# Two interleaved decoder streams on one core: another merged order of the steps, another table of constant matmuls

## The chip, the cores and the metric

The kernel runs on one core of a Trainium2 chip. The metric is the device time of one execution in microseconds, lower is better. A core has five engines that run their own instruction lists in order and meet through semaphores: TensorE (PE in the profile, its weight loads PEld), VectorE (DVE), ScalarE (ACT), GpSimd (POOL) and SyncE (SP), which here only issues transfers.

## The reference, cut to what matters

Two post-norm decoder layers over x of 4 x 512 x 256 in f32. Each batch row goes through six sublayers, each followed by a residual sum and a layer norm:

```python
x = _layernorm(x + _L0_attn_ref(x, Wk, Wq, Wv))                  # causal softmax attention
x = _layernorm(x + _L0_xattn_ref(x, ctx, ctx, mask, ...))        # masked cross attention, own norm
x = _layernorm(x + _L0_ffn_ref(x, k0, k1, k2, s0, s1, s2))       # three dense layers of +1/-1 weights
x = _layernorm(x + _L1_attn_ref(x, Wqkv, ..., proj))             # performer: relu features, causal sums
x = _layernorm(x + _L1_xattn_ref(x, ctx, ctx, Wi_w, ...))        # mLSTM: gated, decayed scores
x = _layernorm(x + _L1_ffn_ref(x, w1, conv_w, conv_b, w2))       # quantized dense, conv over tokens, silu, dense
```

The batch rows are independent of one another. Only the weights are shared.

## The kernel before

**Streams and rounds.** The four batch rows are worked on as two streams, a and b, in two rounds: stream a takes rows 0 and 2, stream b rows 1 and 3. Each stream has its own buffers and its own four of the eight PSUM banks. A third program, p, prepares the weights (on POOL and SP it is called w).

**Programs and steps.** On each engine a stream is a Python generator that yields the name of a step and then emits its instructions. The names are the sublayer and the tile: `self.*` and `cross.*` (the attentions; for each of four row tiles `score`, `turn`, which transposes the probabilities, and `product`), `sign.*` (the dense layers: `sign.xT`, `sign.a0` to `a7`, `sign.b0` to `b7`, `sign.c0` to `c3`), `perf.*` (performer), `mlstm.*` and `quant.*` (the last sublayer: `quant.turn`, `row1`, `hidden0` to `hidden7`, `taps`, `topT`, `row2`, `down0` to `down3`). DVE takes row maxima, norms, half of the bank reads and all of the rounding; ACT takes the exponentials, silu and the other bank reads.

**The order.** `weave` merges the programs of an engine by a table: "a11 b2 a7" means eleven steps of a, two of b, seven of a. There is a table for each engine, so the instruction order of every engine is written out by hand or by a planner outside of this file:

```python
for turn in turns.split():
    name = turn[0]
    for _ in range(int(turn[1:])):
        ahead[name] = next(programs[name], None)
```

There are 590 steps on PE, 773 on DVE, 522 on ACT, 101 on POOL and 34 on SP. Every engine runs its steps strictly in this order, so a step whose inputs are late holds all that stands behind it, of the other stream too.

**The preparing steps.** `prep.scales` on DVE waits for all four transfers of the sign weights (`sign_in`) and then makes their scale and sign columns in eight small instructions (L1221 to L1235); after four of them it signals `signs_taken`. `prep.w10` to `prep.w17` on ACT (L1831) wait for `sign_in` and `signs_taken` and turn one of eight slices of weights from bytes into f16; `prep.w2` (L1834) is four more such instructions. `prep.w00` and `w01` on DVE do the same for the first layer.

```python
dve.wait_ge(*sign_in.all())
dve.wait_ge(*rows_in.all())
```

**The start of stream a.** PE: `self.q` (L564), `self.v` (L572), `self.score0` (L598, L600), `self.cv0` (values of the cross attention, L572), `self.score1`, `self.turn0` (L607). ACT copies the results of `self.q` (L1876) and of `self.v` (L1881) out of their banks; the banks of `self.v` are those that `self.score1` and `self.turn0` write next. DVE takes the row maximum of a score tile (L1276), ACT then its exponential (L1806 loads the table, L1851), and PE turns it.

**Constant matmuls.** `claim` stands ahead of most PE steps. It waits for the bank and then runs as many 128x512 bf16 matmuls of constants (L550) as the table `KEEP` has for that step. Their result is overwritten by the step itself:

```python
for _ in range(KEEP.get(f"{name} {s.index} {n}", 0)):
    nc.tensor.matmul(u.bank[:, :], identb[:, :], ..., start=True, stop=True)
```

The key is step, stream (0 for a, 1 for b) and round.

## Time and profile before

| what | value |
|---|---|
| time of the runs, median of 3 | 808.02 us (807.7 to 809.53) |
| profiled execution, span from the first to the last instruction | 808.1 us |
| PE matmul busy | 738.1 us, 91% of the span |
| DVE busy | 560.4 us, 69% |
| ACT busy | 347.2 us, 43% |
| mean granted TensorE clock | 0.976 of full |
| TensorE at half clock | six stretches, among them 418.0 to 421.4 us and 721.8 to 732.0 us |

The profile gives no time of its own for the profiled execution beside its span; the span is within 0.1 us of the median of the runs. In the profile a line such as L1276 is a line of the kernel. Both streams and both rounds share the lines, so a step is found by the order of the instructions in the timeline, not by the line alone. The granted clock is a share of full speed: 1.00 is 2.4 GHz, 0.50 is 1.2 GHz.

### The profile page before, as it was taken

How to read it: one execution, taken by the hardware profiler on the slowest of the kernel's cores; microseconds unless marked ns; L12 is line 12 of the kernel's file. 1: busy time of each engine (PE TensorE's matmuls, PEld its weight loads, DVE VectorE, ACT ScalarE, POOL GpSimd, SP SyncE). 2: the span in 40 equal slices, each digit the busy share in tenths (PEclk: the TensorE clock that was granted, in tenths of full speed). 3: DMA queues.
4: the chain of work that ended last, by engine and by line, in shares of the span. 5: the costliest groups of instructions: out<-in, count | busy, mean ns of one | idle time of the engine just before them, and what ended most of it. 6: DMA issues, size and time to landing. Idle time of an engine off the chain costs nothing.

```text
span 808.1 us, 14850 instructions
## 1 busy us (share of the span) xinstructions
PE 738.1 (91%) x5976; PEld 485.7 (60%) x5976; DVE 560.4 (69%) x1405; ACT 347.2 (43%) x640; POOL 166.7 (21%) x249
## 2 busy tenths in 40 slices
PE   9999999989999978689979999999999998978494
PEld 6776565667657745557744576867656676646242
DVE  1558436575457589997899973647546569799887
ACT  3576223333144335565337634242324433485253
POOL 8711003010015030022330020011012513103300
PEclk9999999999999999999999999999999999988698
DMA  9402000000002000032000020000000000000001
GB/s 352 183 12 119 1 1 1 1 2 3 27 1 53 2 27 2 0 106 79 27 0 1 1 78 28 2 1 3 0 2 1 1 2 2 1 1 1 1 1 52
DMA packets 12739, 23.76 MB, mean 29 GB/s; under 512 B 768, under 2 KB 7040, under 8 KB 12416
## 3 DMA queue, kind: packets, MB, share of 16 engines
q1 hardware_dynamic: 12672, 22.82, 8.2%
q8 instruction: 47, 0.77, 0.4%
q14 instruction: 20, 0.16, 0.1%
HBM read 20.72 MB, written 2.10 MB: 28 GB/s over the span
## 4 chain that ended last, share of the span: by engine, by line
PE 73%; DVE 17%; ACT 4%; issue 2%; POOL 2%; DVEq 0%; ACTq 0%; POOLq 0%
PE bank L754 14%; PE bank L572 7%; PE bank L564 5%; PE bank L598 5%; PE bank L619 4%; PE bank L852 4%; PE bank L1104 3%; PE bank L764 3%; PE bank L740 3%; PE bank L833 2%; DVE work L1771 2%; PE bank L799 2%; PE bank L702 2%; PE bank L557 1%; PE bank L875 1%
## 5 line engine op out<-in xcount | busy, mean ns | idle before, releaser
L2160 POOL TENSOR_TENSOR rstd<-rstd,minus_half 128x2 f32<-128x2 f32 x56 | 43.1, 771 | 467.8 <-DVE rstd L1201 467.6
L754 PE MATMUL bank<-work,f0w 128*128 128x512 f16 x512 | 114.0, 379 | 0.0
L754 PEld LDWEIGHTS bank<-work,f0w 128*128 128x128 f16 x512 | 49.7, 98 | 59.5 <-issue 1.9
L1937 ACT ACTIVATE work<-bank 128x512 f16<-128x512 f32 x64 | 37.0, 596 | 83.7 <-PE bank L754 70.9
L1411 DVE SCALAR_TENSOR_TENSOR work<-bank,work 128x512 f16<-128x512 f32 x64 | 42.3, 685 | 35.3 <-ACT work L1937 35.2
L619 PE MATMUL bank<-work 128*128 128x256 f32 x208 | 50.2, 383 | 0.7 <-DVE work L1308 0.7
L1975 ACT ACTIVATE work<-bank 128x512 f32<-128x512 f32 x32 | 19.1, 596 | 72.6 <-PE bank L852 72.5
L1276 DVE TENSOR_REDUCE small<-bank 128x1 f32<-128x512 f32 (+3 forms) x32 | 18.8, 588 | 41.8 <-PE bank L600 41.7
L619 PEld LDWEIGHTS bank<-work 128*128 128x128 f32 x208 | 37.6, 190 | 6.8 <-issue 1.2
L1494 DVE TENSOR_TENSOR work<-bank,upper 128x512 f32<-128x512 f32 x32 | 22.0, 688 | 24.4 <-PE bank L852 24.3
L852 PE MATMUL bank<-work 64*128 64x128 f32 x512 | 37.2, 285 | 0.2 <-DVE work L1494 0.2
L852 PEld LDWEIGHTS bank<-work 64*128 64x128 f32 x512 | 31.1, 187 | 9.1 <-issue 8.1
L1195 DVE BATCH_NORM_STATS2 stats<-y 128x6 f32<-128x256 f32 x96 | 35.8, 414 | 0.6 <-ACT y L1915 0.5
L2226 POOL TENSOR_TENSOR small<-small,minus_half 128x16 f32<-128x16 f32 x8 | 24.2, 3028 | 55.1 <-DVE small L1652 55.1
L1962 ACT ACTIVATE work<-bank 128x512 f32<-128x512 f32 x40 | 21.3, 597 | 26.0 <-PE bank L799 25.9
L1104 PE MATMUL bank<-work,f0w 128*128 128x512 f32 x64 | 31.3, 613 | 0.2 <-DVE work L1719 0.2
L1851 ACT ACTIVATE work<-bank,small 128x512 f32<-128x512 f32 (+3 forms) x32 | 19.5, 608 | 27.4 <-DVE small L1280 17.8
L564 PE MATMUL bank<-xT,perf_w 128*128 128x512 f32 x64 | 29.9, 599 | 1.5 <-ACT work L1962 0.9
L598 PE MATMUL bank<-ctxT,work 128*128 128x512 f32 x64 | 30.3, 595 | 0.0
L764 PE MATMUL bank<-f0w,work 128*128 128x256 f16 x256 | 29.2, 273 | 0.0
L550 PE MATMUL bank<-bar_upper,identb 128*128 128x512 bf16 x80 | 25.7, 412 | 3.2 <-ACT work L1962 2.0
L2084 ACT ACTIVATE work<-work 128x512 f32<-128x512 f32 x32 | 19.5, 627 | 19.9 <-DVE work L1771 19.8
(307 smaller groups left out, 1698.1 us busy)
## 6 DMA issues: line engine op xcount, KB each, us to landing
work<-in_mask SPq DMA_DIRECT2D x4, 1024.0 KB, 7.0
xT<-in_xT SPq DMA_DIRECT2D x4, 512.0 KB, 4.0
ctxT<-in_ctxT SPq DMA_DIRECT2D x4, 512.0 KB, 4.7
perf_w<-in_k SPq DMA_DIRECT2D x3, 512.0 KB, 11.7
perf_w<-in_perf_w SPq DMA_DIRECT2D x1, 1536.0 KB, 6.2
x<-in_x SPq DMA_DIRECT2D x2, 512.0 KB, 11.7
ctx<-in_w SPq DMA_DIRECT2D x2, 512.0 KB, 13.8
work<-in_w SPq DMA_DIRECT2D x1, 1024.0 KB, 16.1
```

Source lines behind the costliest of these rows:

```text
L564: ins = nc.tensor.matmul(u.bank[:, :], weights[:, k, c0:c0 + P], src[:, k, :], start=(k == 0), stop=(k == NC - 1))
L572: ins = nc.tensor.matmul(u.bank[:, j * C:(j + 1) * C], src[:, k, t * P:(t + 1) * P], weights[:, k, c0:c0 + C], start=(k == 0), stop=(k == ...
L598: nc.tensor.matmul(u.bank[:, 0:width], s.a_qT[:, k, t * P:(t + 1) * P], keys[:, k, 0:width], start=(k == 0), stop=False)
L619: ins = nc.tensor.matmul(u.bank[:, 0:C], s.probT[:, t % 2, j * P:(j + 1) * P], v[:, j, :], start=(j == 0), stop=(j == tiles - 1))
L754: ins = nc.tensor.matmul(u.bank[:, :], f0w1[:, k, m * P:(m + 1) * P], s.h1[part][:, k, :], start=(k == 0 and part == 0), stop=(k == NF - 1 ...
L764: ins = nc.tensor.matmul(u.bank[:, 0:C], s.h2[part][:, k, t * P:(t + 1) * P], f0w2[:, k, :], start=(k == 0 and part == 0), stop=(k == NF - ...
L852: ins = nc.tensor.matmul(u.bank[:, here], s.kf[rows, pair, here], s.qf[rows, pair, here], start=(i == 0), stop=True, tile_position=(PM * i ...
L1104: ins = nc.tensor.matmul(u.bank[:, :], taps[:, j, k, :], s.flat[j % 4][:, k:k + T], start=(k == 0), stop=(k == 1))
L1195: m = vec.mark(nc.vector.bn_stats(s.stats[:, t, :], src[:, t, :]))
L1411: low_part(what, m, dst, number + m, lambda o, x, hi: nc.vector.scalar_tensor_tensor(out=o, in0=x, scalar=0.0, in1=hi, op0=ALU.max, op1=AL ...
L1937: nc.scalar.activation(dst[0][:, m, :], u.bank[:, :], ACT.Relu).then_inc(s.high_made.sem, 1)
L2160: nc.gpsimd.tensor_tensor(s.rstd[:, two], s.rstd[:, two], minus_half[:, 0:2], ALU.pow).then_inc(s.rstd_made.sem, 1)
```

## The change

The tables `TURNS` (five strings) and `KEEP` are replaced. No other line changes. Each stream's own steps stay in the same order on each engine, with the same instructions and the same waits; what changes is how the streams and the preparing program are merged, and how many constant matmuls run ahead of which step: 80 in all before, 56 after.

The places that matter for what follows:

- DVE: `prep.scales` stood after the first eight steps of a, behind `self.score3`. It now is the very first step, ahead of a's `self.score0`.
- ACT: `prep.w10` stood after the first eight steps of a. It now stands between a's `self.q` and `self.v`, and `prep.w11` between a's `self.score0` and `self.score1`. `prep.w15` and `w16` now stand between a's `cross.q1` and `cross.score0`, `w17` behind that, and `prep.w2` between a's `cross.score2` and `cross.turn1`.
- PE: b's `self.q` and `self.v` stood between a's `self.score3` and `self.turn2`. Now `self.q` of b stands behind a's `self.product1`, and `self.v` of b behind a's `cross.xT0`. b's `self.cv0`, `score1`, `turn0` and `cv1` move from around a's `cross.q0` and `cross.xT1` to behind a's `cross.product1` and `cross.product3`.
- SP: a's xT goes ahead of the folding weights; the sign weights keep their place, behind the same nine transfers. a's mask goes ahead of b's ctxT.
- Both orders have the same steps done on PE when stream a comes to `sign.b4` of round 0, to `cross.score2` of round 1, to `perf.state.1` of round 1 and to `quant.hidden1` of round 1. Between the first two, b is up to 10 steps further ahead against a in the first half (a in `perf`) and up to 11 steps further behind in the second (a in `mlstm` and `quant`).
- PE, end of round 1: a's `quant.topT` now stands behind b's `mlstm.cols`, not ahead of it.
- DVE, end of round 1: a's `quant.q5` moves from ahead of b's `mlstm.ratio0` to behind b's `mlstm.stats0`; a's `quant.down3` and second `quant.stats` move from among b's `quant.conv2` to `conv3` to either side of b's `quant.amax2`.
- `KEEP` of b in round 1 changes from 38 to 20: 10 to 3 ahead of `quant.topT`, 12 to none ahead of `quant.down0`.

```diff
--- before.py
+++ after.py
@@ -35,48 +35,49 @@
 TURNS = {
     "tensor":
-        "a11 b2 a7 b2 a1 b2 a1 b1 a13 b3 a1 b1 p1 a2 b2 a7 b1 a2 b1 a2 b1 a15 b1 a3 b1 a2 b1 a2 b2 a1 b1 a1 b2 a1 b1 a1 "
...
-        "a1 b18 a1 b1 a1 b22",
+        "a13 b1 a5 b1 a2 b1 a10 b1 a3 b4 p1 a1 b5 a2 b2 a2 b1 a21 b1 a6 b1 a2 b1 a1 b1 a1 b1 a1 b1 a1 b1 a2 b1 a1 b7 "
...
+        "b1 a1 b1 a3 b3 a1 b1 a5 b1 a2 b1 a1 b1 a1 b5 a1 b16 a1 b2 a1 b20",
     "vector":
-        "a8 p1 a9 p1 a1 b1 a13 p1 a1 b3 a3 b1 a13 p1 a2 b1 p1 a4 b2 a2 b2 a4 b1 a1 b3 a1 p1 b2 p1 a2 b1 a2 b2 a11 b7 a1 "
...
-        "a1 b3 a1 b2 a1 b5 a1 b2 a1 b1 a1 b1 a2 b10 a1 b3 a1 b1 a1 b6 a1 b3 a2 b2 a3 b2 a1 b19 a1 b17",
+        "p1 a12 p1 a20 b1 a3 p1 a1 b1 a10 b2 p1 a1 b1 a1 b1 a1 b1 p1 b2 a2 b1 a2 b1 a2 b1 a1 b3 a3 b1 p1 a1 b2 a3 p1 "
...
+        "b3 a2 b6 a1 b1 a1 b1 a1 b10 a1 b6 a2 b2 a1 b4 a2 b1 a1 b4 a1 b11 a1 b7 a1 b1 a1 b16 a1 b1",
     "scalar":
-        "a8 p1 a4 b2 p2 a2 p2 a4 p1 b1 a1 p2 a3 p1 a2 p1 a1 p2 a4 p2 a2 b1 a1 p2 a1 p1 a2 b2 a2 b1 a4 b1 a4 b3 a2 b1 a2 "
...
-        "a2 b2 a4 b1 a1 b1 a6 b12 a1 b2 a3 b3 a4 b23 a1 b4 a1 b4",
+        "a1 p1 a2 p1 a7 p1 a2 p1 a3 b1 a4 p1 a1 p2 a1 p1 a2 p1 a2 p1 a3 p1 b1 p2 a1 p2 a2 b1 p1 a1 p1 a1 b1 a1 b6 a2 "
...
+        "b1 a1 b3 a1 b1 a1 b1 a1 b1 a1 b1 a1 b1 a1 b28 a2 b1",
     "gpsimd":
-        "a7 b2 a5 b5 a5 b2 a1 b3 a4 b1 a1 b4 a2 b1 a2 b1 a1 b2 a2 b1 a2 b1 a4 b2 a1 b2 a1 b5 a4 b4 w1 b1 a1 b1 a5 b10 a2 "
-        "b2",
+        "a7 b2 a3 b2 a2 b3 a6 b2 a2 b1 a1 b1 a2 b3 a1 b2 a1 b2 a2 b4 a4 b1 a1 b1 a2 b1 a1 b1 a2 b3 a1 b3 a3 b1 a1 b1 "
+        "a1 w1 b3 a1 b1 a4 b10 a2 b2",
     "sync":
-        "w1 a2 w1 a1 w3 b1 w2 b1 a1 b1 w1 b1 a5 b1 a1 b1 a1 b6 a2 b1",
+        "a1 w1 a2 w4 b1 w2 a1 b3 w1 a4 b1 a3 b6 a1 b1 a1 b1",
 }
 KEEP = {
-    "perf.xT1 0 0": 1, "perf.fk.1 0 0": 1, "perf.ft.1 0 0": 1, "perf.score2.1 0 0": 1, "mlstm.head6 0 0": 1,
-    "quant.turn0 0 0": 1, "quant.turn1 0 0": 2, "quant.hidden0 0 0": 3, "cross.turn1 0 1": 1, "sign.early 0 1": 4,
-    "perf.spread.1 0 1": 1, "mlstm.head3 0 1": 1, "mlstm.state2 0 1": 1, "mlstm.out3 0 1": 1, "quant.turn0 0 1": 1,
-    "self.score0 1 0": 1, "self.turn2 1 0": 1, "self.product1 1 0": 1, "self.product3 1 0": 2, "perf.state.0 1 0": 1,
-    "perf.spread.0 1 0": 3, "perf.fk.1 1 0": 5, "perf.ft.1 1 0": 2, "perf.state.1 1 0": 2, "perf.out1 1 0": 1,
-    "mlstm.xT0 1 0": 2, "cross.q1 1 1": 1, "perf.qk.0 1 1": 1, "perf.ft.1 1 1": 2, "perf.state.1 1 1": 3,
-    "mlstm.head0 1 1": 3, "mlstm.head4 1 1": 1, "quant.turn0 1 1": 3, "quant.turn1 1 1": 1, "quant.topT 1 1": 10,
-    "quant.row2 1 1": 1, "quant.down0 1 1": 12
+    "perf.qk.0 0 0": 2, "quant.hidden1 0 0": 1, "quant.hidden2 0 0": 2, "quant.hidden3 0 0": 1,
+    "quant.hidden6 0 0": 1, "self.turn2 0 1": 1, "cross.turn2 0 1": 1, "perf.v0 0 1": 1, "quant.taps6 0 1": 2,
+    "quant.topT 0 1": 3, "perf.fk.0 1 0": 1, "perf.state.0 1 0": 3, "perf.spread.0 1 0": 1, "perf.fq.1 1 0": 3,
+    "perf.ft.1 1 0": 1, "perf.state.1 1 0": 4, "perf.spread.1 1 0": 3, "mlstm.out0 1 0": 1, "quant.turn0 1 0": 3,
+    "quant.turn1 1 0": 1, "perf.fk.1 1 1": 1, "perf.ft.1 1 1": 1, "perf.state.1 1 1": 3, "perf.score0.1 1 1": 1,
+    "mlstm.cols 1 1": 3, "mlstm.head1 1 1": 1, "mlstm.head3 1 1": 1, "mlstm.head5 1 1": 1, "mlstm.state2 1 1": 1,
+    "quant.row1 1 1": 1, "quant.hidden1 1 1": 2, "quant.topT 1 1": 3, "quant.down3 1 1": 1
 }
```

## Rows read from the trace of the kernel before

**Rows 1.** The page: span and busy time of the engines

```profile
span 808.1 us, 14850 instructions
...
PE 738.1 (91%) x5976; PEld 485.7 (60%) x5976; DVE 560.4 (69%) x1405; ACT 347.2 (43%) x640; POOL 166.7 (21%) x249
```

**Rows 2.** The page: shares of the chain that ended last

```profile
PE 73%; DVE 17%; ACT 4%; issue 2%; POOL 2%; DVEq 0%; ACTq 0%; POOLq 0%
```

**Rows 3.** Stretches: us, busy PE, PEld, DVE, ACT, POOL, clock, DMA share, GB/s

```profile
8.40:67.30 58.90, 58.90 (x265) 43.75 (x266) 29.87 (x93) 34.48 (x73) 30.59 (x40) 1.00 0.50 189
...
120.00:280.00 160.00, 156.37 (x1435) 103.58 (x1435) 96.95 (x230) 57.75 (x111) 26.14 (x40) 1.00 0.04 11
280.00:360.00 80.00, 62.03 (x724) 41.83 (x718) 72.55 (x172) 40.43 (x67) 14.23 (x23) 0.98 0.10 30
...
399.00:447.00 48.00, 41.79 (x203) 23.12 (x202) 45.67 (x120) 26.47 (x48) 9.42 (x18) 0.96 0.04 12
447.00:700.00 253.00, 245.36 (x2282) 166.63 (x2281) 160.89 (x402) 94.21 (x176) 44.80 (x68) 1.00 0.03 10
...
740.00:770.00 30.00, 16.13 (x83) 9.58 (x84) 25.86 (x76) 7.09 (x11) 8.16 (x12) 0.72 0.00 1
```

**Rows 4.** Timeline of SP: start, us, issue of a transfer

```profile
6.77 0.43 SPq L2258 DMA_DIRECT2D work<-in_k  x1
```

**Rows 5.** DMA issues: KB of one, median us from issue to landing

```profile
work<-in_k SPq DMA_DIRECT2D x1, 256.0 KB, 12.7
```

**Rows 6.** Timeline of 15 to 28 us: start, us, engine, line, operation [idle before]

```profile
15.53 0.59 ACT L1881 COPY work<-bank 128x512 f32<-128x512 f32 x1 [1.14 <-PE bank L572]
...
16.11 0.29 DVE L1276 TENSOR_REDUCE small<-bank 128x1 f32<-128x128 f32 x1 [12.56 <-PE bank L600]
16.42 1.28 ACT L1806 ACT_TABLE_LOAD   x1 [0.31 <-DVE small L1276]
...
17.71 0.37 ACT L1851 ACTIVATE work<-bank,small 128x128 f32<-128x128 f32 x1
...
18.53 0.28 PE L607 MATMUL bank<-ident,work 128*128 128x128 f32 x1
...
24.96 0.16 DVE L1221 TENSOR_SCALAR s_cols<-rows_all 128x2 f32<-128x2 f32 x1
...
25.76 1.23 ACT L1831 ACTIVATE f0w<-perf_w,signed 128x1024 f16<-128x1024 uint8 x1
...
26.65 0.28 DVE L1235 SCALAR_TENSOR_TENSOR centring<-mlstm_block,ident 128x128 f32<-128x128 f32 x1
```

**Rows 7.** Timeline of ACT, 45 to 58 us

```profile
45.28 2.36 ACT L1831 ACTIVATE f0w<-perf_w,signed 128x1024 f16<-128x1024 uint8 x2
...
54.94 2.17 ACT L1834 ACTIVATE f0w<-work 128x512 f16<-128x512 uint8 x4
```

**Rows 8.** Waits of PE up to 80 us: total us, times, longest

```profile
PE bank L557 <- ACT x L1822: 1.3, 1, 1.3
```

**Rows 9.** Stretches around two stops of PE, columns as in rows 3

```profile
413.20:417.30 4.10, 0.00 (x0) 0.03 (x1) 3.96 (x17) 1.07 (x2) 2.03 (x3) 1.00 0.00 0
418.00:421.40 3.40, 3.40 (x14) 1.67 (x13) 3.23 (x13) 1.15 (x2) 1.03 (x9) 0.50 0.01 2
...
721.80:732.00 10.20, 8.61 (x47) 6.29 (x48) 8.63 (x19) 8.03 (x15) 2.80 (x4) 0.50 0.01 2
```

**Rows 10.** Waits of PE, 280 to 360 us

```profile
PE bank L1074 <- DVE small L1522: 3.0, 2, 1.7
...
PE bank L1126 <- DVE work L1740: 1.5, 1, 1.5
```

**Rows 11.** Timeline of PE, 719 to 764 us

```profile
723.39 1.09 PE L1126 MATMUL bank<-ident,work 128*128 128x128 f32 x4 [4.03 <-DVE work L1740]
...
752.84 0.82 PE L1144 MATMUL bank<-f1w,work 128*128 128x256 bf16 x3 [7.43 <-DVE work L1764]
```

**Rows 12.** Groups of instructions on PE: the constant matmuls

```profile
L550 PE MATMUL bank<-bar_upper,identb 128*128 128x512 bf16 x80 | 25.7, 412 | 3.2 <-ACT work L1962 2.0 <-ACT work L1958 1.1
```

40 rows, old and new, of the table TURNS are left out of this document.

## The prediction, on record before the result

> **What bounds the kernel now.** I read the page first: PE is busy in 91% of the span, DVE in 69% [rows 1], and 73% of the chain that ended last lies on PE [rows 2]. The reader is to see that PE is the bound on the whole, so a microsecond in which PE newly stands still is a microsecond of span, unless a later stop shrinks by it.
>
> The second view, busy time by stretch, says where PE has stops to give back [rows 3]. From 8.4 to 67.3 us it has none (58.90 of 58.90). From 120 to 280 us it has 3.6 us in 160, and from 447 to 700 us 7.6 us in 253. The stops are in the stretches where DVE is full: 280 to 360 us (PE idle 80.0 - 62.0 = 18.0 us, DVE idle 80.0 - 72.6 = 7.4 us), 399 to 447 us (PE idle 6.2 us, DVE idle 2.3 us) and 740 to 770 us (PE idle 13.9 us, DVE idle 4.1 us). There DVE is the bound in fact, and another order gives back at most what DVE stands idle. Time lost before 120 us therefore goes through PE undiminished to 280 us at least.
>
> As only the order changes, I then read in which step each engine stood, by the timeline, and asked of every moved step what it waits for and what is now queued behind it.
>
> **The start.** `prep.scales` is now the first step of DVE. It waits for the sign weights. Their last transfer is issued at 6.77 us [rows 4] and lands 12.7 us later [rows 5], at 19.5 us. In the new order of SP the same nine transfers are ahead of it, so that time stays. Before, DVE had its first row maximum at 16.11 us, and met `prep.scales` at 24.96 us, long after the landing, so that it waited for nothing [rows 6]. Now DVE stands until 19.5 us, then needs for the step what it took before, from 24.96 to 26.65 + 0.28 = 26.93, that is 2.0 us, and is free at 21.5 us. Queued behind it is the whole of stream a on DVE, and behind that a's exponentials on ACT and transposes on PE.
>
> ACT is held too. `prep.w10` stands ahead of the copies of a's `self.v` and waits for `signs_taken`, which comes about 0.6 us into the DVE step (estimate, four of its eight instructions), at 20.1 us. It takes 1.23 us [rows 6], to 21.3 us. The two copies follow, 0.59 us each [rows 6], to 22.5 us. Then come the table load of 1.28 us and the exponential of 0.37 us with its read-out [rows 6]: 24.4 us. PE turned this tile at 18.53 us [rows 6], and now does so at about 24.5 us. All its work up to there is the same, and nothing of b is placed ahead, since b's `self.q` now comes after a's `self.product1`. That is **6.0 us** of new idle time of PE, in two pieces: about 4.1 us until the first copy frees the bank of `self.score1`, and about 1.6 us behind that, the rest being small change. Bounds: 5.3 us, if only DVE's delay from 16.1 to 21.4 us passed through, and 7.5 us, if the two slices of `prep.w11` and the later copies of `cv1` add one more ACT slice of 1.23 us.
>
> With b's first steps moved behind, a's chain has less cover in the next 40 us, while the ACT slices stand closer to it. `prep.w15` and `w16` (2.36 us [rows 7]) now stand ahead of the exponential of `cross.score0`. ACT's copies of `cross.q1` end about when the score tile ends, so the exponential comes some 0.7 us after the time at which PE could use it. `prep.w2` (2.17 us [rows 7]) now stands ahead of ACT's copy for `cross.product1`: about 0.5 us. `cross.q1` has only b's `self.score0` between it and `cross.xT1`: about 0.4 us, and small pieces of 0.4 us around `self.turn2`. Together **2.0 us**; bounds 0 (all hidden) and 4.5 us (both ACT groups fully exposed). In return, the stop of 1.3 us at a's `sign.xT0` [rows 8] should go, since four steps of b now stand ahead of it: **-1.3 us** (bounds 0 and -1.3).
>
> A stop of 4.1 us also costs clock. After the idle 4.10 us at 413.2 the granted clock was 0.50 from 418.0 to 421.4 us, and after the stop that ended at 723.4 us it was 0.50 from 721.8 to 732.0 us [rows 9, 11]. One stretch like the shorter takes 3.4 x 0.5 = 1.7 us of PE's work, of which some falls into the waits that follow: **+1.0 us** (bounds 0 and 5.1, the longer stretch). The Trainium skill (TensorE: Matmul & The Clock Gate, "HAM oscillation — how this bites in real kernels") counts the penalty as half of the throttled time; by that alone this term would be 1.7 us and the sum 0.7 us more, while what these rows show is the clock, not how much of the loss is hidden.
>
> **The middle.** From 120 to 399 us b is first further ahead of a, then further behind. What this gives back shows in the waits of PE from 280 to 360 us: 3.0 us at the token rows (L1074) and 1.5 us at a's `quant.topT` (L1126) [rows 10], where before little or nothing of b stood between and now two to eight microseconds of b's performer do. Against that, b's `mlstm.cols` and its later steps lose cover (7 us of a's PE work between it and `mlstm.raw1`, now about 3), and DVE is the bound here. Of the 4.5 us I take a little over half: **-2.5 us**. Bounds: -7.4 us, all of DVE's idle time there [rows 3], and +4.5 us, the same waits once more. From 399 to 700 us PE has 6.2 + 7.6 us idle, the kinds of pairing are the same, and I take nothing, with -3 and +3 as bounds, about half of the latter.
>
> **The end.** At 723.4 us PE had waited 4.03 us for DVE's last maximum of a's `quant.topT`, with b's `mlstm.cols` queued behind it [rows 11]. b is the stream that ends last, and its gate steps now go first on PE and on DVE: about -1.0 us, at most -4.0. a's `quant.q5` behind b's ratios: -1.0 us, one of eight such steps. The waits of 7.43 us at a's `quant.down0` [rows 11] only move, since DVE is busy with b's norm there. Against it a's second `quant.stats` now stands between b's `quant.amax2` and `quant.q0`, with about 0.5 us sticking out of the wait for the token row. Together **-1.5 us** (bounds -4.5 and +2).
>
> **The constant matmuls.** 24 fewer of 412 ns [rows 12] are 9.9 us less PE work, but almost all stood in stops, where PE was waiting anyway, so I cost their absence at nothing. What hides it is the wait itself, b's chain of rounding at the end above all. Without them the clock may fall there: another short half-clock stretch of 1.7 us, of which b's last matmuls see a part; this is in the bound of +2 above.
>
> **The sum.** 6.0 + 2.0 - 1.3 + 1.0 - 2.5 - 1.5 = +3.7 us on the profiled span of 808.1 us [rows 1], which is within 0.1 us of the median of the runs: **811.8 us**.
>
> **The rivals.**
> *The middle repays more than the start costs (faster).* The place is 280 to 447 us, the mechanism that DVE finds work of the other stream where it now idles. It decides from 7.8 us on, since start less end is 7.7 - 1.5 = 6.2 us and 1.6 more are needed. With all of DVE's idle time there, 7.4 + 2.3 = 9.7 us [rows 3], the time is 808.1 + 6.2 - 9.7 = 804.6 us. For it speaks that several PE waits of 1 to 2 us get cover, against it that DVE would have to be 100% busy. Chance 0.22.
> *The start is absorbed (no change).* If the later stops of PE are mere lengths of PE's lead over DVE, then 6.2 us less of the 18.0 us idle from 280 to 360 us [rows 3] would be needed. DVE is as late as PE by then, and that speaks against it: 808. Chance 0.12.
> *The new order is worse in the full stretches too.* Steps of a and b are merged more finely on DVE, and b's `mlstm` chain loses 4 to 5 us of cover at two steps. With the upper ends of the middle (+4.5) and of the clock (+4.1 more), less some overlap of 2: 811.8 + 7.0 + 4.1 - 2 = 821 us. Fewer constant matmuls belong here: the stretch of 10.2 us at half clock [rows 9] once more is 5.1 us. Chance 0.18.
> *The wait at the start isn't there.* If the sign weights landed before 16.1 us, the 6.0 us vanish and the time is 805.8 us. All transfers of the start are seen to land in the order of issue, and 12.7 us after issue is far from the 9.3 that this needs [rows 4, 5]. The Trainium skill (DMA: Bandwidth & Descriptors, "Queues, rings and completion order") says that completion is not first-in-first-out per issuing engine; that alone would allow it, the landings here don't show it. Chance 0.03.
> *As summed.* Chance 0.45.
>
> **How the numbers follow.** About 0.2%, 1.6 us, is what a measurement tells from no change. Faster: 0.22 of the first rival, nearly all of the fourth, less the part of the first that ends within 1.6 us: 0.22. Same: 0.12 and a little of the sum's lower edge, together 0.14. Slower: 0.64. The range takes in the first rival's 804.6 and most of the third: 804 to 820 us. That of the likeliest case alone is 809.5 to 815.5.
>
> **What would show it.** In the changed profile: DVE's first L1276 at 21.5 us instead of 16.1, with L1221 ahead of it at 19.5; ACT's first L1831 at 20.1 us; PE idle about 6 us between 17 and 25 us, with a stretch at half clock behind it; `cross.product3` of a some 5 to 6 us later; the wait at L1126 near 340 us gone; PE's wait at 723 us shorter. The prediction is wrong if PE's idle time from 280 to 447 us falls by more than 8 us, if DVE's idle time from 120 to 447 us grows, or if half-clock stretches come up in the middle, where there are two short ones now.

## The result, and the profile after

The changed kernel takes 814.91 us in the median of 6 runs (811.2 to 817.62), the one before, on the same chip, 808.52 us (807.68 to 809.53). The ratio is 1.0073, with a 95% interval from 1.0059 to 1.0087: slower by about 6 us. The profiled execution is the fastest of the six, 811.2 us with a span of 809.9 us. In every run for which both are on record the span is 1.2 to 1.3 us shorter than the time, so the profiled execution of the kernel before, with its span of 808.1 us, took about 809.4 us (an estimate), some 0.9 us more than the median of its runs. A second measurement of the same kernel gave 815.01 us (810.82 to 820.86), and there the profiled execution took 816.56 us with a span of 815.3 us. The two profiles together show what one does not.

The page of the profiled execution, span and busy time, then the shares of the chain that ended last, against [rows 1, 2]:

```profile
span 809.9 us, 14751 instructions
...
PE 726.5 (90%) x5899; PEld 487.4 (60%) x5952; DVE 564.8 (70%) x1405; ACT 348.8 (43%) x640; POOL 162.7 (20%) x249
...
PE 68%; DVE 18%; issue 7%; ACT 3%; DMA 2%; POOL 1%; SPq 1%; DVEq 0%; ACTq 0%; POOLq 0%
```

One thing has to be read here before any busy time is compared. The kernel has 24 matmuls fewer than 5976, which is 5952, and that many weight loads are in the trace, but only 5899 matmuls: 53 records are missing. So PE's busy time is too low, and "issue" in the chain may be too high. Below, PE's progress is read by the time at which both kernels begin a step with the same work behind them. Where idle time is summed, it is taken from an experiment with the same order whose records are all there, and a wait in this profile can be two shorter ones around a matmul that is missing.

The start, by the timeline of DVE, ACT, PE and POOL, against [rows 6]:

```profile
19.77 0.80 DVE L1222 TENSOR_SCALAR s_cols<-rows_all 128x2 f32<-128x2 f32 x1 [16.23 <-DMA work<-in_k]
20.61 0.97 DVE L1224 TENSOR_SCALAR s_cols<-s_cols 128x2 f32<-128x2 f32 x1
21.61 0.15 DVE L1226 TENSOR_SCALAR signed<-s_cols 128x1 f32<-128x1 f32 x1
21.68 0.14 DVE L1227 TENSOR_SCALAR signed<-s_cols 128x1 f32<-128x1 f32 x1
21.75 1.05 DVE L1228 TENSOR_TENSOR s_cols<-s_cols,rows_all 128x2 f32<-128x2 f32 x1
22.83 0.16 DVE L1230 TENSOR_TENSOR s_cols<-s_cols 128x1 f32<-128x1 f32 x1
23.02 0.21 DVE L1232 TENSOR_SCALAR s_cols<-s_cols,rows_all 128x1 f32<-128x1 f32 x1
23.15 1.00 DVE L1236 SCALAR_TENSOR_TENSOR centring<-mlstm_block,ident 128x128 f32<-128x128 f32 x1
24.07 0.28 DVE L1277 TENSOR_REDUCE small<-bank 128x1 f32<-128x128 f32 x1
...
21.93 1.24 ACT L1832 ACTIVATE f0w<-perf_w,signed 128x1024 f16<-128x1024 uint8 x1 [8.74 <-DVE signed L1227]
23.07 1.05 ACT L1882 COPY work<-bank 128x512 f32<-128x512 f32 x2
...
23.69 2.07 PE L599 MATMUL bank<-xT,work 128*128 128x256 f32 x4 [5.39 <-ACT work L1882]
...
26.27 0.45 PE L608 MATMUL bank<-ident,work 128*128 128x128 f32 x1 [0.40 <-ACT work L1852]
```

```profile
19.46 1.08 POOL L2130 TENSOR_SCALAR_AFFINE_SELECT head_row<-head_row 8x1024 bf16<-8x1024 bf16 x1
20.61 0.94 POOL L2129 MEMSET head_tile<- 8x1024 bf16 x1
21.69 1.08 POOL L2130 TENSOR_SCALAR_AFFINE_SELECT head_tile<-head_tile 8x1024 bf16<-8x1024 bf16 x1
22.92 1.08 POOL L2125 TENSOR_SCALAR_AFFINE_SELECT head_tile<-head_tile 16x1024 bf16<-16x1024 bf16 x1
```

(Lines of the changed kernel are one higher than before.) The reader is to see three things. DVE stands until the sign weights land, as predicted. Then the step lasts from 19.77 to 24.07 us, 4.3 us instead of 2.0: four of its eight instructions take 0.80 to 1.05 us, and each of the four ends within 0.15 us of the end of one of POOL's instructions (20.54, 21.55, 22.77, 24.00). And PE stands 5.39 + 0.40 us and turns its first tile at 26.27 instead of 18.53 us.

The same stretches as [rows 3], then four of the stretches at half clock (columns as there):

```profile
8.40:67.30 58.90, 52.19 (x217) 37.19 (x219) 24.82 (x68) 27.98 (x54) 28.97 (x38) 0.94 0.43 163
...
280.00:360.00 80.00, 66.07 (x774) 48.09 (x782) 67.10 (x159) 38.58 (x66) 13.04 (x29) 0.96 0.09 28
399.00:447.00 48.00, 41.22 (x196) 24.19 (x199) 43.98 (x112) 26.03 (x49) 9.15 (x19) 0.93 0.00 1
...
21.90:28.70 6.80, 4.61 (x12) 3.33 (x13) 3.40 (x7) 5.52 (x9) 6.19 (x7) 0.50 1.03 387
288.10:295.00 6.90, 5.22 (x64) 4.50 (x66) 5.04 (x21) 1.09 (x2) 1.73 (x11) 0.51 0.01 2
417.90:424.70 6.80, 5.47 (x26) 3.91 (x25) 5.88 (x21) 1.33 (x3) 0.70 (x1) 0.50 0.01 2
789.90:803.60 13.70, 9.22 (x36) 4.71 (x37) 12.33 (x34) 4.98 (x8) 1.13 (x2) 0.50 0.00 0
```

At half clock PE is for 61.0 us of the span, 38.5 us before (the mean granted clock is 0.962 and 0.976). The second profile of the same kernel has 74.6 us (0.954). It has one stretch that the first has not, here in the two executions, the slower one first:

```profile
665.60:686.10 20.50, 16.57 (x125) 12.31 (x128) 13.58 (x42) 4.93 (x10) 4.63 (x11) 0.50 0.00 1
```

```profile
665.60:686.10 20.50, 14.98 (x235) 11.31 (x240) 18.95 (x59) 6.28 (x13) 4.83 (x12) 1.00 0.01 2
```

How far the changed kernel is behind the one before, at the start of steps of PE that have the same work done ahead of them in both orders:

| step of stream a | before, us | after, us | difference | after, second profile |
|---|---|---|---|---|
| `self.turn0`, round 0 | 18.5 | 26.3 | +7.7 | +7.8 |
| `sign.b4`, round 0 | 99.2 | 106.3 | +7.0 | +6.4 |
| same instructions done | 236.5 | 239.8 | +3.3 | +2.6 |
| `sign.xT0`, round 1 | 417.3 | 417.4 | +0.1 | -0.9 |
| `perf.state.1`, round 1 | 547.9 | 548.7 | +0.7 | -1.4 |
| `quant.hidden1`, round 1 | 690.4 | 690.8 | +0.4 | +5.6 |
| end of the span | 808.1 | 809.9 | +1.8 | +7.2 |

The third row is no step of a: up to there PE has started the same instructions in both orders, counted by line and shape, the constant matmuls left out.

That is the whole result in one table. The start loses 7 us. The stretch from 106 to 417 us wins all of them back, 3.7 us up to 240 us and 3.2 us behind it. The end loses 1.4 us. In the second profile a half-clock stretch of 20.5 us behind 665 us loses 7.5 us more (second profile against first: -2.2 us ahead of it, +5.3 behind it). Of the twelve runs of this kernel in both measurements, eight have a mean granted clock of 0.956 or less; only one of the eight has a profile, so where the clock fell in the others is not shown.

The waits of PE from 280 to 360 us, against [rows 10]:

```profile
PE bank L853 <- DVE work L1476: 2.9, 1, 2.9
...
PE bank L1127 <- DVE work L1741: 0.6, 1, 0.6
...
PE bank L1075 <- DVE small L1523: 0.2, 1, 0.2
```

The waits at the token rows (L1075, 3.0 before) and at `quant.topT` (L1127, 1.5 before) are nearly gone. At b's `perf.score0.0` (L853) there is a new one of 2.9 us, which ends at 289.5 us, and the half clock sets in during it, at 288.1 us. (With all records there, in the kernel with three more matmuls below, it is 2.8 us in two waits.)

The timeline of PE at the end, against [rows 11]:

```profile
723.00 0.82 PE L551 MATMUL bank<-bar_upper,identb 128*128 128x512 bf16 x3 [2.42 <-ACT work L2006]
...
727.19 1.11 PE L1127 MATMUL bank<-ident,work 128*128 128x128 f32 x4 [1.34 <-DVE work L1741]
...
760.75 0.58 PE L1086 MATMUL bank<-identb,work 128*128 128x128 bf16 x4 [16.16 <-DVE work L1693]
...
794.71 6.68 PE L1145 MATMUL bank<-f1w,work 128*128 128x256 bf16 x24 [2.40 <-DVE work L1765]
801.61 1.91 PE L1155 MATMUL bank<-f1w,work 128*128 128x256 bf16 x8 [0.22 <-issue]
```

and the last two steps in the kernel before:

```profile
791.06 2.75 PE L550 MATMUL bank<-bar_upper,identb 128*128 128x512 bf16 x12
793.65 0.49 PE L1144 MATMUL bank<-f1w,work 128*128 128x256 bf16 x3
...
798.21 1.29 PE L1144 MATMUL bank<-f1w,work 128*128 128x256 bf16 x9 [0.43 <-DVE work L1764]
799.33 1.04 PE L1154 MATMUL bank<-f1w,work 128*128 128x256 bf16 x8
```

Before, twelve constant matmuls of 2.75 us stood ahead of b's last `quant.down0`, and the 32 matmuls of the last product ran at full clock, waiting for DVE: 793.65 to 800.37 us, 6.7 us. After, they run at half clock and wait for nothing: 794.71 to 803.52 us, 8.8 us.

### The profile page after: what moved, and what is told of

The parts are those of the page before. It is cut to its first block, busy times and chain, and to the rows that moved or that the text cites. A ratio compares the mean times of both kernels' runs of the same rounds, so it can differ in the third digit from the quotient of the medians.

```text
span 809.9 us, 14751 instructions
## 1 busy us (share of the span) xinstructions
PE 726.5 (90%) x5899; PEld 487.4 (60%) x5952; DVE 564.8 (70%) x1405; ACT 348.8 (43%) x640; POOL 162.7 (20%) x249
## 4 chain that ended last, share of the span: by engine, by line
PE 68%; DVE 18%; issue 7%; ACT 3%; DMA 2%; POOL 1%; SPq 1%; DVEq 0%; ACTq 0%; POOLq 0%
PE bank L755 14%; PE bank L573 5%; PE bank L565 5%; PE bank L853 4%; PE bank L620 4%; PE bank L599 3%; PE bank L741 3%; PE bank L765 3%; PE bank L1105 2%; PE bank L800 2%; PE bank L558 2%; PE bank L834 2%; PE bank L863 2%; DMA work<-in_k 2%; PE bank L876 2%
## 5 line engine op out<-in xcount | busy, mean ns | idle before, releaser
L1495 DVE TENSOR_TENSOR work<-bank,upper 128x512 f32<-128x512 f32 x32 | 22.1, 690 | 33.0 <-PE bank L853 32.9
L853 PE MATMUL bank<-work 64*128 64x128 f32 x512 | 38.1, 289 | 7.7 <-issue 3.7
L853 PEld LDWEIGHTS bank<-work 64*128 64x128 f32 x512 | 31.9, 191 | 9.5 <-issue 9.0
L1277 DVE TENSOR_REDUCE small<-bank 128x1 f32<-128x512 f32 (+3 forms) x32 | 18.7, 585 | 23.7 <-PE bank L601 17.3
L1852 ACT ACTIVATE work<-bank,small 128x512 f32<-128x512 f32 (+3 forms) x32 | 19.4, 607 | 31.1 <-DVE small L1281 19.5
L1590 DVE TENSOR_TENSOR work<-work 128x512 f32<-128x512 f32 x32 | 25.5, 815 | 4.2 <-ACT work L2040 3.9
## 6 DMA issues: line engine op xcount, KB each, us to landing
ctx<-in_w SPq DMA_DIRECT2D x2, 512.0 KB, 13.7
```

The costliest lines, as they stand in the source:

```text
L853: ins = nc.tensor.matmul(u.bank[:, here], s.kf[rows, pair, here], s.qf[rows, pair, here], start=(i == 0), stop=True, tile_position=(PM * i ...
```

## The experiments

Twelve measurements, one of them of the changed kernel itself, each in five rounds against the kernel before. That kernel's median was 809.2 to 809.5 us in these measurements. Ratios are to it.

**Four stretches, one new at a time.** At some points both orders have, on every engine, exactly the same steps done. There the tables can be cut: after 41, 295 and 519 steps of PE (66, 398 and 690 us), 57, 360 and 638 of DVE, 54, 256 and 443 of ACT, 7, 46 and 87 of POOL, 20 and 30 of SP. Each of these kernels takes one stretch of every table from the new order and the rest from the old, and the constant matmuls with their steps. The cut for the first, with each table up to it:

```diff
@@ TURNS, first stretch (s_head) @@
 "tensor":
-    "a11 b2 a7 b2 a1 b2 a1 b1 a13 b1 ...
+    "a13 b1 a5 b1 a2 b1 a10 b1 a3 b4 ...
 "vector":
-    "a8 p1 a9 p1 a1 b1 a13 p1 a1 b3 a3 b1 a13 p1 ...
+    "p1 a12 p1 a20 b1 a3 p1 a1 b1 a10 b2 p1 a1 b1 a1 ...
 "scalar":
-    "a8 p1 a4 b2 p2 a2 p2 a4 p1 b1 a1 p2 a3 p1 a2 p1 a1 p2 a4 p2 a2 b1 a1 p2 a1 p1 ...
+    "a1 p1 a2 p1 a7 p1 a2 p1 a3 b1 a4 p1 a1 p2 a1 p1 a2 p1 a2 p1 a3 p1 b1 p2 a1 p2 a2 b1 p1 a1 p1 a1 b1 ...
```

Start, up to 66 us. 

> The new order only up to about 66 us (PE's first 41 steps, DVE's first 57, ACT's first 54, POOL's 7, SP's 20), the order of before behind it, with the constant matmuls of each stretch's own table. Theory (the stretches add): the stop of PE from 18 to 24 us and the loss of 6 to 7 us pass through, since DVE is as late as PE in the middle: 814 to 816 us. Rival (the later stops of PE absorb it, the middle's gain in the changed kernel was only this absorption): 808 to 810 us.

Measured: 819.29 us (816.98 to 820.48), ratio 1.0104 (1.0076 to 1.0132). Slower than even the theory had it. The profiled execution, the fastest of its runs, is 8.6 us behind at every step from `sign.b4` of round 0 (107.9 instead of 99.2 us) to `mlstm.out0` (281.3 instead of 272.7 us), and 7.6 us at the end. The stops of 18 us between 280 and 360 us gave back 0.5 us of it. The rival is out for the old order of the middle.

Middle, 66 to 398 us. 

> The order of before up to 66 us and from about 398 us on, the new order between. Theory (the stretches add): the 7 us which the changed kernel had won back at cross.product2 of round 1 are a gain of the new order itself, 801 to 803 us. Rival (they were only the later stops absorbing the start): 807 to 809 us.

Measured: 810.86 us (809.44 to 815.45), ratio 1.0019 (0.9999 to 1.0039). Outside the ranges of both. The profile shows a cost of the cut itself: PE meets a new stop at 67.3 us, with half clock from 70.0 to 76.8 us behind it:

```profile
71.04 0.56 PE L586 MATMUL bank<-s_sum,ones 128*128 128x2 f32 x2 [3.70 <-DVE s_sum L1248]
```

and a half-clock stretch from 315.8 to 326.0 us which the changed kernel does not have. From `sign.b4` (+3.6 us) to `cross.product2` of round 1 (+1.8) it still wins 1.8 us with 10.2 us more at half clock than the changed kernel. All of the gain up to 236.5 us is there (-0.1 us at that point, 3.7 us won). So it neither shows nor rules out the 7 us; the start put back, below, does that.

Late, 398 to 690 us. 

> The new order only from about 398 to 690 us. In the changed kernel's profile this stretch took 0.6 us more than before. Theory: 808 to 809.5 us. Rival (it is worse by itself, and the changed kernel's slower runs lose here): 810 to 813 us.

Measured: 820.98 us (819.79 to 822.1), ratio 1.0131 (1.0105 to 1.0157). Far outside the ranges of both. Here too the cut costs: DVE and ACT of the old order are not as far at 398 us as the new one takes them to be.

```profile
403.21 1.12 PE L609 MATMUL bank<-ident,work 128*128 128x128 f32 x4 [4.58 <-ACT work L1853]
```

The kernel is 6.0 us behind at `sign.xT0` of round 1. At 667.7 us of the kernel before, another point with the same instructions done, it is 7.7 us behind, and 12.6 us at `quant.hidden1`, with half clock from 674.8 to 691.9 us between the two. The spread of the changed kernel may come from there, and its second profile, below, was taken for that.

End, from 690 us. 

> The new order and the new constant matmuls only from about 690 us on (12 fewer matmuls). Theory: the end costs the 1.5 to 2 us of the changed kernel's profile and, in most runs, 2 to 4 us more by a lower clock: 810 to 813 us. Rival (the lower clock of the other runs comes from elsewhere, the end is neutral): 808 to 809.5 us.

Measured: 811.91 us (811.42 to 813.77), ratio 1.0028 (1.0011 to 1.0045). In the theory's range. But the twelve runs lie within 2.4 us: the spread of the changed kernel does not come from the end.

The four ratios add up to 2.8%, the change is 0.7%. A single new stretch measures its seams too, as the stops at 67.3 and 398.6 us show, and with them where the clock falls.

**The changed kernel once more.** 

> The changed kernel once more, for another profile. Theory: its runs spread (811 to 818 us) because a stretch at half clock comes up in some of them and not in others, the candidate being the stops at 665 to 669 us of round 1, behind which the late-stretch kernel had half clock from 674.8 to 691.9 us and lost about 6 us. Median 814 to 816 us. Rival: the start or the end differ from run to run instead.

Measured: 815.01 us (810.82 to 820.86). The second profile is shown above: half clock from 665.6 to 686.1 us, behind the stop at 662.7 us and in what follows at 665.2 us, with +7.5 us over the stretch. The theory holds and the rival falls, for these two executions: the second profile is 0.7 us ahead over the start and loses 0.2 us more at the end (1.6 against 1.4).

**The start put back.**

```diff
@@ the changed kernel @@
 "vector":
-    "p1 a12 p1 a20 b1 ...
+    "a8 p1 a4 p1 a20 b1 ...
 "scalar":
-    "a1 p1 a2 p1 a7 p1 a2 p1 ...
+    "a8 p2 a2 p1 a2 p1 ...
```

> The changed kernel with prep.scales on DVE and prep.w10, w11 on ACT back behind the first eight steps of a, all else as changed. Theory (the start's stop passes through, and what the middle won back is its own): 7 to 8.5 us less than the changed kernel's 815, so 806 to 808.5 us. Rival (the middle's gain was the start's delay absorbed): 811 to 814 us.

Measured: 807.66 us (802.67 to 814.71), ratio 0.9992 (0.9968 to 1.0016). It is 7.3 us less than the changed kernel, and in the profiled execution 7.2 us less at `sign.b4` and 8.4 us less from 288 us to the end (span 801.5 us), the last 1.2 us by a half-clock stretch that is shorter there. At `sign.b4` it is level with the kernel before (-0.2 us), and at `sign.xT0` of round 1 it is 8.3 us ahead. The 7 us of the middle are a gain of the new order and not the start's delay absorbed. The new order from 40 us on is no worse than the old one: its best run is 5 us faster than the old one's best. Its runs spread over 12 us, with a mean granted clock of 0.968 in the fastest and 0.950 in the slowest.

**One step moved in the kernel before.**

```diff
@@ the kernel before @@
 "vector":
-    "a8 p1 a9 p1 a1 b1 ...
+    "p1 a17 p1 a1 b1 ...
```

> The kernel before, with one step moved: prep.scales is the first step of DVE; ACT, PE and all else as before. Theory (DVE's late row maxima alone hold stream a, by 21.5 - 16.1 = 5.4 us, and nothing behind gives it back): 5.5 to 7 us slower, 814.5 to 816.5 us. Rival (much of the head's 8 to 9 us is ACT's slices of weights ahead of the copies of self.v): 811 to 813.5 us.

Measured: 819.62 us (817.6 to 824.0), ratio 1.0133 (1.0112 to 1.0154). More than expected, with ACT's slices left where they were, and the rival falls. PE turns its first tile at 26.30 us, the same time as in the changed kernel, after one stop of 7.79 us, and the stretch at half clock behind it is 10.2 us long. At `sign.b4` the kernel is 10.6 us behind and stays so up to 660 us. So ACT's slices ahead of the copies cost nothing at this turn, and DVE's step alone gives the whole delay of it. Its length of 4.6 us is what the prediction had wrong.

**The same step, with POOL standing aside.** POOL builds its head rows and head tiles in the background at this time. Here it waits for the end of DVE's step before the second of its selects of 16x1024, and so stands from 17.1 to 21.0 us.

```diff
@@ the kernel above @@
         for r in range(0, 3 * 32, 32):
+            if r == 32:
+                pool.wait_ge(*centring_made.at(0))
             pool.wait_ge(*gps.mark(nc.gpsimd.affine_select(
```

> The kernel of scales_first (prep.scales first on DVE, 819.6 us) in which POOL waits for the end of that step before its second head_tile select, and so stands from about 18.3 us to it. Theory (three or four of the step's eight small instructions last 0.8 to 1.1 us instead of 0.16 to 0.3 because each waits out an instruction of POOL, which ends at the same time): the step takes 2.0 us or less instead of 4.6, PE turns the first tile at about 23.7 us instead of 26.3, and the kernel is 2.5 to 5 us faster, 815 to 817 us. Rival (the instructions are slow for another reason, the transfers that land then or a first use): the step stays at 4.6 us, 819 to 820 us.

Measured: 817.18 us (816.02 to 819.59), ratio 1.0095 (1.0077 to 1.0114), 2.4 us less. The step in the timeline of DVE:

```profile
19.49 0.17 DVE L1222 TENSOR_SCALAR s_cols<-rows_all 128x2 f32<-128x2 f32 x1 [15.94 <-DMA work<-in_k]
19.70 0.17 DVE L1224 TENSOR_SCALAR s_cols<-s_cols 128x2 f32<-128x2 f32 x1
...
20.03 0.15 DVE L1228 TENSOR_TENSOR s_cols<-s_cols,rows_all 128x2 f32<-128x2 f32 x1
...
20.54 0.28 DVE L1236 SCALAR_TENSOR_TENSOR centring<-mlstm_block,ident 128x128 f32<-128x128 f32 x1
20.74 0.28 DVE L1277 TENSOR_REDUCE small<-bank 128x1 f32<-128x128 f32 x1
```

From 19.49 to 20.82 us, 1.3 us instead of 4.6, and PE's first turn at 22.94 instead of 26.30 us. The four instructions that took 0.8 to 1.1 us take 0.15 to 0.28. The transfers land as before. The theory holds, and with it the cause is shown. Its time for the turn (23.7 us) was even too late. The kernel is 6.1 us behind at `sign.b4` where the one above was 10.6, with 3.4 instead of 10.2 us at half clock at the start. The median lies just above the theory's 815 to 817 us, and its gain of 2.4 us just below the 2.5 to 5 expected.

**The constant matmuls of the end.** The 2 x 2 of order and table from 690 us on.

```diff
@@ KEEP of the end, old against new @@
-    "mlstm.head0 1 1": 3, "mlstm.head4 1 1": 1, "quant.turn0 1 1": 3, "quant.turn1 1 1": 1, "quant.topT 1 1": 10,
-    "quant.row2 1 1": 1, "quant.down0 1 1": 12
+    "quant.taps6 0 1": 2, "quant.topT 0 1": 3, "mlstm.cols 1 1": 3, "mlstm.head1 1 1": 1, "mlstm.head3 1 1": 1,
+    "mlstm.head5 1 1": 1, "mlstm.state2 1 1": 1, "quant.row1 1 1": 1, "quant.hidden1 1 1": 2, "quant.topT 1 1": 3,
+    "quant.down3 1 1": 1
```

New order, old table. 

> The order of before up to 690 us, the new order from there on, but with the constant matmuls of before in the end too (80 in all; 10 and 12 ahead of b's last quant.topT and quant.down0). Theory (the end's 2.5 us are the half clock behind the missing matmuls): 808.5 to 810 us. Rival (they are the new order's stop of 16 us at 745 us): 811 to 813 us.

Old order, new table. 

> The order of before everywhere, and only the constant matmuls of the end replaced by the new table's (68 in all, 3 instead of 10 and none instead of 12 at b's last topT and down0). Theory (missing matmuls cost the clock): 811 to 813 us, with half clock from about 787 us on. Rival (they only filled waits): 808.5 to 810 us.

Measured: 811.46 us, ratio 1.0039 (1.0026 to 1.0051), for the new order with the old table, and 810.81 us, ratio 1.0021 (1.0012 to 1.0030), for the old order with the new table. Both new is the 1.0028 from above. So neither theory is right alone: the new table costs about 1.6 us in the old order and little in the new one (811.91 against 811.46 us), and the new order costs 2.2 us with the old table. In the profile of the new order with the old table PE is 1.9 us behind at 740.7 us of the kernel before, 1.3 us at 770 us, and the span is 2.1 us longer (810.2 against 808.1 us). Its last product, b's `down0` to `down3`, takes 8.1 us, 3.3 of them at half clock, with 2.1 us of waits for DVE. Under the new table (the end experiment) it takes 8.8 us, all but 0.1 at half clock, and waits for nothing: most of what the clock gives, DVE takes back there.

**Three matmuls ahead of the stop at 663 us.**

```diff
@@ KEEP of the changed kernel @@
+    "perf.fq.1 1 1": 3
```

> The changed kernel with three more constant matmuls, ahead of b's perf.fq.1 of round 1, where PE stands 1.4 us at 663 us. Theory (the clock falls to half in most runs from 665 to 686 us, because of the short stops there; three matmuls of 0.41 us keep it up): the spread shrinks and the median is 811 to 812.5 us. Rival (other stops hold it down, or the fall is elsewhere in most runs): 814 to 816 us.

Measured: 816.59 us (814.21 to 820.52), ratio 1.0099 (1.0079 to 1.0120). The theory falls. Of the stop of 1.4 us at 663 us, 0.75 us are left. The next one, 1.75 us in the profiles of the changed kernel, is here two of 0.73 and 0.63 us around a constant matmul whose record is missing there. So there is no stop above 1 us left from 417 to 724 us, and the clock is nevertheless at half from 673.1 to 683.3 us.

**The parts put together.** The start as in "the start put back", the three matmuls, and order and table of before from 690 us on. 

> The start put back as in start_back, the new order from there to 690 us, the three matmuls ahead of b's perf.fq.1, and from 690 us on the order and the constant matmuls of before. Theory (the parts add: start -7.5, clock at 665 us -3 to -4, end -2 from 815): 800.5 to 803 us, faster than both. Rival (a seam or the clock eats it): 805 to 809 us.

Measured: 808.25 us in the median of eleven runs (801.46 to 810.57), ratio 0.9972 (0.9947 to 0.9997). A twelfth run took 4078 us, at a granted clock of 1.00; why is not known, and it is left out. The median is in the rival's range. The profiled execution (span 809.3 us) has half clock from 309.3 to 323.0 us, with PE 96% busy in it, and again from 667.7 to 681.4 us:

```profile
309.30:323.00 13.70, 13.12 (x98) 10.38 (x101) 8.89 (x20) 5.66 (x11) 0.00 (x0) 0.50 0.00 1
```

The first of them costs 5.5 us: up to 288 us the kernel keeps step with the start put back, which has the same stops from there to 310 us and full clock behind them, and at `quant.topT` it is that much behind it. It is barely faster than the kernel before in the median, but its best runs are 6 us faster than any of it.

## Why the prediction was right, and where its terms were off

The forecast was +3.7 us and 811.8 us. The profiled execution shows +1.8 us and the median run about +6 us. The direction, the place and the mechanism of the loss were right, and several sizes were not. That the sum came near is in part luck: against the first profile its parts are off by -0.7 us (start), -4.4 (middle), +0.3 (399 to 700 us) and +2.9 (end), and these cancel to -1.9. The 811.8 us were also the span of one execution taken for a time; as a time the forecast is about 813.1 us (809.4 + 3.7).

**The start, 6.0 + 1.0 + 2.0 - 1.3 = +7.7 us; measured +7.0 us** at `sign.b4`, the first step with the same work behind it. The pieces:
- The stop: predicted 6.0 us idle, measured 5.8 (5.39 + 0.40). The start of the step was right (19.5 us; 19.77 measured). The step that failed is that DVE "needs for the step what it took before", 2.0 us: it took 4.3 us and, with POOL aside, takes 1.3 us. DVE's first row maximum came at 24.07 us instead of 21.5, and PE's turn at 26.27 instead of 24.5. The idle time is not larger because part of the longer wait is hidden: the tile between the two stops runs at half clock (2.07 + 0.31 us instead of 1.03 + 0.22), and PE came to the stop 0.5 us late.
- ACT's part: its L1832 came at 21.93 us instead of 20.1, being behind the same slow DVE instructions, and had no cost of its own at the turn: with ACT's order left alone it comes at the same time (26.30 us).
- The clock: predicted +1.0 us, with one short stretch of 3.4 us. Measured 6.8 us at half clock in one profile and 3.4 in the other, and these two differ by 0.7 us over the start. In the 6.8 us PE is busy for 4.61 us, so the term was about 2.3 us there (an estimate, half of the busy time). A stretch of 10.2 us came with the longer stop of 7.8 us. "After the stop" was also misread: at the start the clock falls at 21.9 us, inside the stop from 18.3 to 23.7 us, and in the kernel before it fell at 721.8 us, inside the one from 719.4 to 723.4 us [rows 9, 11].
- Less cover: predicted +2.0 us. One small stop is there, 0.4 us at `cross.q1` (52.19 us), as predicted, and none else. ACT's slices were hidden nearly whole.
- The stop of 1.3 us at `sign.xT0` [rows 8] is gone, as predicted. PE comes to this step at 77.18 us without a wait.

**Nothing absorbs it.** That a loss ahead of 120 us goes through PE and DVE undiminished was the assumption against the rival of no change. The experiment with only the start new shows it: +8.6 us, constant over 170 us, and 8.1 us past the 18 us of stops in the middle.

**The middle, -2.5 us; measured -6.9 us** (+7.0 to +0.1). This is the term that was mis-sized most, and most of the miss is one of place. The prediction looked for the gain from 280 to 360 us alone. But 3.7 us of it are won before 240 us, in a stretch that had only 3.6 us of idle time. Two of PE's waits there, at the performer's scores, are gone:

```profile
174.74 1.14 PE L799 MATMUL bank<-work,perf_w 32*128 32x512 f32 x8 [1.40 <-DVE y L1508]
...
177.64 1.14 PE L799 MATMUL bank<-work,perf_w 32*128 32x512 f32 x8 [0.63 <-ACT work L1962]
```

In the kernel with three more matmuls, whose 5955 records are all there, PE's idle time from `sign.b4` to this point is 1.8 us instead of 3.6, and its busy time 1.7 us less. Two constant matmuls fewer are 0.8 us of that at most. Why the same instructions then take about 1 us less in the new order is not shown.

Behind 240 us 3.2 us are won, against the 2.5 predicted. The waits named are gone, as predicted: 3.0 to 0.2 us at the token rows, 1.5 to 0.6 us at `quant.topT`. These 3.7 us are more than the whole gain; the other waits and 3.4 us more at half clock took the rest. Here the stretches between the same instructions, of the kernel before and of the one with three more matmuls:

```profile
236.50:417.30 180.80, 157.75 (x1514) 112.69 (x1511) 149.94 (x378) 88.31 (x164) 44.36 (x57) 0.99 0.11 33
```

```profile
239.70:416.90 177.20, 158.30 (x1512) 113.60 (x1510) 155.09 (x385) 88.24 (x164) 44.23 (x65) 0.98 0.11 34
```

DVE's idle time in them falls from 30.9 to 22.1 us. So the first rival had the mechanism right for this part, but neither the place of the rest nor enough to pay for the start. In windows of fixed time it looks otherwise, since the kernels stand at different work there. From 280 to 360 us DVE's idle time grew from 7.4 to 12.6 us:

```profile
280.00:360.00 80.00, 68.47 (x785) 48.58 (x784) 67.38 (x161) 38.59 (x66) 12.66 (x29) 0.96 0.10 28
```

Of the three signs of being wrong, two were not met: from 120 to 447 us DVE's idle time fell from 80.3 to 75.7 us, and PE's from 280 to 447 us fell by 5.2 us, not by more than 8. The third, half clock in the middle, was met: two stretches of 6.8 us instead of two of 3.4, and one more in the second profile. Order and constant matmuls of the middle were changed together in every experiment; from `sign.b4` to `sign.xT0` of round 1 there are 28 such matmuls before and 26 after, so their number is no rival, while their places are not tested alone.

**From 399 to 700 us, nothing; measured +0.3 us in the first profile, +6.5 in the second** (+0.1 to +0.4, and -0.9 to +5.6). In the first profile the waits cancel out, as argued. What was missing is the clock: this stretch was read as safe because the profile of before had no half clock in it after 421 us, and the bounds of -3 and +3 us were for waits alone. The sign "or if half-clock stretches come up in the middle" was the right one.

**The end, -1.5 us; measured +1.4 us.** The wait at 723 us was to become 1 us shorter. It became two waits, 2.42 and 1.34 us, together 3.8 instead of 4.03. The constant matmuls were costed at nothing with a bound of +2 us. Taken out of the old order they cost 1.6 us. Taken out of the new order they cost under 0.5 us, but there the order has its own price of 2.2 us. What was "another short half-clock stretch of 1.7 us" in the prediction is one of 13.7 us, and the last product took 8.8 instead of 6.7 us.

**The missing 4 us of the median.** Of the 4.6 us between +1.8 and +6.4, 0.9 are the kernel before, whose profiled execution took more than its median (see above). The other 3.7 us are the changed kernel, whose profiled execution was its fastest. They go with the granted clock, 0.962 in that run and 0.950 to 0.958 in the five others, which one profile cannot show. With stretches that are there in one execution and not in another of the same order, the cost is 7.5 us for 20.5 us, and between the combined kernel and the start put back 5.5 us for 13.7 us. The Trainium skill (TensorE: Matmul & The Clock Gate, "HAM oscillation — how this bites in real kernels") counts half of the throttled time. The runs here give 0.37 and 0.40 us for each microsecond of it, a little less. A likely reason is that PE also has waits in such a stretch (it is busy for 16.57 of the 20.5 us and 13.12 of the 13.7).

**What stays open.** Why the clock falls at 665 to 690 us in some executions and not in others of the same kernel. Stops above 1 us are not needed for it, as the three matmuls show, and they are not enough for it: the start put back has the same stops as the changed kernel there (from 656 to 661 us) and full clock behind them. The order of before runs at full clock there in its own profile, and yet has a stretch at half in the profile of the one moved step (680.4 to 694.1 us, 5.3 us lost). That a late start brings it is not shown: with its start unchanged, 2 of the 23 runs of the kernel before in the first four experiments took 814.5 us at a granted clock of 0.967; all the others took at most 810.0 us, at 0.972 to 0.979. They have no profile, so where the clock fell is not known. Nor is it shown why the new order of the end costs 2.2 us; only the place of most of it is, between 690 and 741 us.

## What to carry to other kernels

A preparing step that waits for a late transfer belongs behind the work that can run without it, whatever it waits for elsewhere: one such step at the head of DVE's queue cost 7 to 11 us (6 with POOL aside), and nothing downstream absorbed it. When one engine's background work (here POOL's constants) runs beside a step that is moved onto the path, take the step's cost from both sides of that neighbour, since eight tiny instructions cost 1.3 us alone and 4.6 us beside it. Judge an order by several executions and by its time at half clock, not by its idle time alone. Compare two orders at points where the same work is done, not in windows of the same time, and do not add up measurements of spliced parts.

## What the runs showed of the hardware that was not expected

- POOL held DVE up at instructions of a few elements. Beside POOL's selects and memsets of 0.94 to 1.08 us, a 128x2 f32 tensor-scalar took 0.80 to 1.10 us instead of 0.17, a tensor-tensor with both inputs in SBUF 1.05 instead of 0.15, a 128x128 one with a scalar 1.00 instead of 0.28. The 128x1 tensor-scalars beside the same POOL instructions took 0.14 to 0.21 us. The Trainium skill (SBUF — State Buffer, "Who interferes with whom") says that a vector instruction in a mode that uses both ports contends with GpSimd, and so does one with two inputs in SBUF while GpSimd's instruction reads SBUF, and that whoever issues first has the shared ports for the whole instruction. The traces agree: the four held instructions end within 0.15 us of one of POOL's. The sign of it was in the trace of the kernel before, in the middle of the same step, where one instruction was held instead of four, and it was read as the instruction's own time:

```profile
25.49 0.80 DVE L1227 TENSOR_TENSOR s_cols<-s_cols,rows_all 128x2 f32<-128x2 f32 x1
```

- The clock fell to half (309.3 to 323.0 us in the combined kernel, PE 96% busy in it) after 20 us in which PE was busy for 15.7 us and no stop was longer than 1.2 us.
- The same kernel had 61.0 us at half clock in one execution and 74.6 us in another, and its times spread by 10 us (810.8 to 820.9). The runs of the kernel before spread by 2 us beside these, and by 7 us (807.9 to 814.6) beside the first four experiments.
